# Two merge lanes become three, and the constant rows and first tokens go ahead of the first norm, in a four-layer transformer kernel

## The chip, the cores and the metric

The kernel runs on one core of one Trainium2 chip. The metric is the device time of one execution in microseconds, taken as the median over several runs; the program before the change has 2537.3 us (3 runs, 2535.52 to 2537.45). One further execution was recorded by the hardware profiler.

## The reference, cut to what is computed

Input is `x` (2 batches, 1024 tokens, 256 channels), a conditioning vector for each batch and a context of 77 tokens. Four layers follow each other, all with 256 channels and 16 heads of 16:

```python
x = L0(x)   # modulated norm, window attention (8 windows of 128 tokens, rolled by 64), projection;
            # norm, top-16 cross attention over the 77 context tokens; norm, SwiGLU MLP
x = L1(x)   # norm, attention over the context as prototypes, 3 experts, gate, x + gate * routed
x = L2(x)   # modulated norm, rotary full self attention with a block mask; cross attention; GELU MLP
x = L3(x)   # modulated norm, full self attention without a mask; cross attention; GELU MLP
```

The full self attention of L2 and L3, the part that matters most here, is for each batch and head

```python
attn = softmax(einsum('bqhd,bkhd->bhqk', q, k) * scale)      # 1024 x 1024, L2: masked first
out = einsum('bhqk,bkhd->bqhd', attn, v).reshape(B, N, 256) @ W_proj
```

## The kernel before, in words

**Stages and lanes.** The program is made of stages (`Norm`, `Parts` for the q and k projections, `Values`, `Attention`, `OutProject`, `Mlp`, `Experts` ...). Each stage has one generator for each of the five engines (tensor = PE, vector = DVE, scalar = ACT, pool = POOL, sync = the DMA queue SP). A generator issues an instruction or a few and yields. `phases` (L2855) lists the stages in columns, the lanes: lane 0 holds the attentions, lane 1 the other batch's projections, norms and MLPs, and SP has a third lane of loads. For each engine `merge` (L244) takes turns among the lanes' generators by a string in `ORDER` (L192): each character is a number of yields to take from the next lane in turn (`Z` adds 61 and stays on the lane). So the strings are the complete order of each engine, written out by hand or by a planner; nothing is decided at run time but semaphore waits.

**Batches.** While batch 0 is in an attention on lane 0, batch 1 is in its dense stages on lane 1, and the other way round.

**A full attention** (`Attention`, L1058, `kind="full"`) works on 8 groups of 2 heads. For a group and each of 32 steps: `max_tile` (L1159) makes a product of 128 queries x 512 keys in one of banks 0 and 1 (L1171), and DVE takes its row maximum (L1303; in the masked layer L1300 adds the mask too). After the 32, the maxima are transposed (L1140), split in two bf16 parts (L1257, L1260) and put by DMA as two more rows into the stacked queries (L1118). Then `exp_tile` (L1181) makes the transposed product with that shift (L1196, mask by L1200) in bank 2 or 3, ACT takes the exponential (L1238) into one of seven buffers, and `pv` (L1203) multiplies four of them with the values into bank 4 (L1224, four strips of the array side by side). After the group ACT copies bank 4 (`finish_copy`, L1027), PE transposes it (`finish_turn`, L1034) and DVE divides by the sums (`finish_out`, L1045, L1051). The turned sums go into a bank of the pair 0 and 1: line 1153 takes `self.bank("max", turns)`. All this is laid out on beats: exponentials begin 40 beats behind the maxima, value products 46, the turn 75; a group begins each 40 beats (masked layer) or 32 (last layer). Each beat ends in a yield of its own, whether or not anything was issued in it.

**The start.** `Start.sync` (L433) issues the DMAs of the condition, `ident`, `cols`, the bias and the first piece of the modulation weights, then all tokens of batch 0 in one DMA (L438), then the weights. `Mods` multiplies the condition with the modulation weights piece by piece (L554). `Norm` takes statistics of eight tiles of 128 tokens (L695, L700), POOL takes one inverse root for all eight (`root_guess`, L666 and L668), DVE refines it (L644 to L651) and normalizes tile by tile (L718), PE transposes each (L740), ACT applies the modulation into `hT` (L782). The window attention rolls the tokens by 64, so its projections (L822) need both halves of `hT`. `StackRows` (L473) fills constant rows (-1, 0, 1 in bf16) of the stacked queries and keys of three buffers, nine fills of 2048 elements, and the ones beside the values, in a single yield, in lane 1 behind the norm.

## Time and profile before

| | |
|---|---|
| median of 3 runs | 2537.3 us |
| profiled execution | 2540.68 us |
| its span, first to last instruction | 2539.4 us |
| granted TensorE clock, mean | 0.951 |
| busy: PE, DVE, ACT, POOL | 2331.7, 1686.7, 1267.6, 384.6 us |
| instructions | 37005 |
| DMA | 160.6 MB |

Busy time is the union of an engine's drawn instructions. Matmuls are pipelined and their ends are modelled, so two that follow each other closely overlap in the drawing, and a short wait can lie under a drawn product. A weight load (PEld) runs ahead of the product it belongs to, so its idle time is partly covered. Idle time of an engine is put down to what ended it.

### The profile page before, as it was taken

To read this page: it belongs to the slowest core of one execution; us is meant where nothing else is said; L and a number is where in the kernel's file an instruction comes from. 1 tells how busy PE (TensorE), PEld (TensorE's weight loads), DVE (VectorE), ACT (ScalarE), POOL (GpSimd) and SP (SyncE) were. 2 spreads that over 40 slices of the span, in tenths; PEclk is the share of its full clock that TensorE was granted. 3 is DMA by queue.
4 is the path that set the end of the run, shared out by engine and by line. 5 is a ranking of instruction groups with operands and counts; after the bars stand their busy time and mean duration, and the time that the engine had idled before them with its cause. 6 is when DMAs were issued, how large, how long until landed. Compare 5 with 4: busy or idle time off the path is not lost.

```text
span 2539.4 us, 37005 instructions
## 1 busy us (share of the span) xinstructions
PE 2331.7 (92%) x13127; PEld 1214.5 (48%) x13127; DVE 1686.7 (66%) x5146; ACT 1267.6 (50%) x2434; POOL 384.6 (15%) x407
## 2 busy tenths in 40 slices
PE   6789789978997989999989999998999989999997
PEld 2566345555554545545444455552344433334554
DVE  5666978676235575567867775758886668884563
ACT  2334445443222314455546655645766637776553
POOL 3011444244121110001110010010001010002021
PEclk8899789999998979999999999997999999999999
DMA  4666440000001140001223100042221042110120
GB/s 161 186 153 203 123 142 24 28 22 5 4 9 33 63 78 18 14 14 26 94 86 101 56 18 13 14 150 75 66 50 21 18 131 88 52 41 11 51 71 17
DMA packets 150925, 160.63 MB, mean 63 GB/s; under 512 B 33391, under 2 KB 120259, under 8 KB 150477
## 3 DMA queue, kind: packets, MB, share of 16 engines
q1 hardware_dynamic: 150740, 158.28, 22.0%
q8 instruction: 103, 1.69, 0.3%
q14 instruction: 82, 0.66, 0.1%
HBM read 97.39 MB, written 60.19 MB: 62 GB/s over the span
## 4 chain that ended last, share of the span: by engine, by line
PE 74%; DVE 13%; ACT 3%; DMA 3%; POOL 2%; issue 2%; SPq 1%; ACTq 0%; DVEq 0%; POOLq 0%
PE bank L1224 10%; PE bank L1196 9%; PE bank L1758 9%; PE bank L1171 9%; PE bank L1781 6%; PE bank L1200 4%; PE bank L822 4%; PE bank L2264 4%; PE bank L2444 3%; PE bank L1678 3%; DVE max L1303 2%; PE bank L2266 2%; PE bank L740 2%; PE bank L1034 1%; DVE stats L695 1%
## 5 line engine op out<-in xcount | busy, mean ns | idle before, releaser
L1238 ACT ACTIVATE work<-bank 128x512 f32<-128x512 f32 (+1 forms) x1216 | 687.6, 596 | 404.8 <-PE bank L1200 199.5
L1300 DVE CUSTOM_DVE_ANT_0 bank<-bank,weights 128x512 f32<-128x512 f32 x512 | 347.3, 702 | 121.3 <-PE bank L1171 119.8
L1171 PE MATMUL bank<-k_stack,q_stack 97*128 97x512 bf16 x896 | 354.6, 401 | 35.8 <-DVE max L1303 17.6
L1303 DVE TENSOR_REDUCE max<-bank 128x1 f32<-128x512 f32 x512 | 334.1, 684 | 72.5 <-PE bank L1171 70.0
L1196 PE MATMUL bank<-q_stack,k_stack 99*128 99x512 bf16 x896 | 339.9, 383 | 7.5 <-ACT work L1238 5.8
L1758 PE MATMUL bank<-hT,weights 128*128 128x512 f32 x512 | 256.4, 612 | 9.8 <-ACT work L1808 4.3
L1171 PEld LDWEIGHTS bank<-k_stack,q_stack 97*128 97x128 bf16 x896 | 88.3, 99 | 250.9 <-DVE max L1303 106.7
L1200 PEld LDWEIGHTS bank<-ident_b,weights 128*128 128x128 bf16 x2048 | 157.8, 97 | 102.0 <-issue 8.5
L1781 PE MATMUL bank<-weights,work 128*128 128x256 f32 x768 | 195.8, 384 | 3.5 <-DVE work L1848 3.2
L1200 PE MATMUL bank<-ident_b,weights 128*128 128x128 bf16 x2048 | 198.1, 218 | 0.0
L1781 PEld LDWEIGHTS bank<-weights,work 128*128 128x128 f32 x768 | 140.8, 190 | 67.4 <-issue 29.5
L822 PE MATMUL bank<-hT,weights 128*128 128x512 f32 x288 | 152.4, 644 | 9.4 <-ACT hT L782 4.7
L1196 PEld LDWEIGHTS bank<-q_stack,k_stack 99*128 99x128 bf16 x896 | 86.9, 98 | 115.9 <-ACT work L1238 73.5
L1290 DVE TENSOR_REDUCE max<-bank 128x4 f32<-128x308 f32 (+1 forms) x192 | 101.8, 544 | 51.4 <-PE bank L1177 50.5
L1224 PE MATMUL bank<-work,weights 128*17 128x512 f32 x1024 | 135.5, 598 | 0.0
L1758 PEld LDWEIGHTS bank<-hT,weights 128*128 128x128 f32 x512 | 92.8, 193 | 88.0 <-issue 57.2
L1224 PE MATMUL bank<-work,v 128*17 128x512 f32 x1024 | 134.7, 598 | 0.0
L2264 PE MATMUL bank<-hT,weights 128*128 128x512 f32 (+1 forms) x240 | 123.6, 627 | 0.5 <-ACT work L2462 0.3
L740 PE MATMUL bank<-ident,work 128*128 128x128 f32 x320 | 73.8, 346 | 48.0 <-DVE work L718 44.1
L1550 POOL TENSOR_TENSOR x<-x,row_consts 128x256 f32<-128x256 f32 x112 | 84.5, 754 | 193.2 <-DMA row_consts<-in_L_b_cproj 176.8
L2444 PE MATMUL bank<-weights,work 128*128 128x256 f32 x384 | 95.7, 385 | 1.0 <-DVE routed L2590 0.4
L2458 ACT ACTIVATE work<-bank,half_anchor 128x512 f32<-128x512 f32 x56 | 38.5, 687 | 114.6 <-PE bank L2266 112.2
(241 smaller groups left out, 3611.6 us busy)
## 6 DMA issues: line engine op xcount, KB each, us to landing
q_stack<-parts_q SPq DMA_DIRECT2D x60, 384.0 KB, 4.1
parts_q<-parts SPq DMA_DIRECT2D x46, 384.0 KB, 2.6
k_stack<-parts_k SPq DMA_DIRECT2D x40, 384.0 KB, 4.9
weights<-parts_q SPq DMA_DIRECT2D x36, 384.0 KB, 3.8
parts_q<-parts SPq DMA_DIRECT2D x46, 256.0 KB, 2.9
parts_k<-parts SPq DMA_DIRECT2D x24, 384.0 KB, 2.6
parts_k<-parts SPq DMA_DIRECT2D x24, 256.0 KB, 3.0
weights<-in_L_e_w SPq DMA_DIRECT2D x12, 512.0 KB, 7.5
```

What stands on the lines that cost most here:

```text
L822: m = pe.e.matmul(bank.ap[:, :], w[:, i, self.col + c * P:self.col + (c + 1) * P], hT[self.b][:, bl, i, :], start=i == 0, stop=i == CC - 1)
L1171: m = pe.e.matmul(bank.ap[:, :], self.q(g)[0:MAX_ROW, h, qt * P:(qt + 1) * P], k_stacks[self.key, g].ap[0:MAX_ROW, h, half * BLK:(half + 1 ...
L1196: m = pe.e.matmul(bank.ap[0:self.nk, :], self.k(g, h, STACK, kt * P), q, start=True, stop=not self.mask)
L1200: m = pe.e.matmul(bank.ap[:, j * P:(j + 1) * P], mask_bias[:, half * TPB + j, kt * P:(kt + 1) * P], ident_b[:, :], start=False, stop=j == ...
L1224: m = pe.e.matmul(o[strip:strip + DV, :], self.v[:, kt, head, :] if self.own else self.v[:, head, :], p[0:self.nk, :], start=kt == 0, stop ...
L1238: ac.e.activation(p.ap[0:self.nk, :], banks[self.key, "exp", g, i].ap[0:self.nk, :], ACT.Exp).then_inc(*probs.tick((self.key, g, i)))
L1300: ve.e.tensor_tensor_reduce(bank[:, :], bank[:, :], mask_bias[:, qt, half * BLK:(half + 1) * BLK], 1.0, -3.4e38, ALU.add, ALU.max, to).the ...
L1303: ve.e.tensor_reduce(to, bank[:, :], AX_X, ALU.max).then_inc(*maxima.tick((self.key, g, i)))
L1758: m = pe.e.matmul(banks[key].ap[:, :], w1[:, k, col:col + P], hT[self.b][:, bl, k, :], start=k == 0, stop=k == CC - 1)
L1781: m = pe.e.matmul(banks[self.key, tp].ap[:, i * C:(i + 1) * C], hid[:, at * P:(at + 1) * P], w2[:, j, :], start=(j == 0 and i == 0), stop= ...
L2264: return pe.e.matmul(out, wt[name][:, k, lo:hi], hT[self.b][:, self.bl, k, :], start=k == 0, stop=False)
L2444: m = pe.e.matmul(banks[key, "acc", ex, pair].ap[:, i * C:(i + 1) * C], hid[:, at * P:(at + 1) * P], wt[f"L1w2_{ex}"][:, j, :], start=(j = ...
```

## The change

- `Start.sync` issues batch 0's tokens as two DMAs of 512 tokens, directly behind the condition and ahead of `ident`, `cols` and the modulation weights.
- Fills of the constant rows write two bf16 values as one f32 pattern (`fill`). `StackRows` stands first in lane 1, ahead of the first norm, with one yield for each fill; the ones beside the values and the context's key rows become a stage `ValueOnes`, behind that norm.
- The first norm of batch 0 takes its inverse root in two halves (`roots=2`); each half's tiles follow its own root.
- In the four full attentions, `FullAttention` keeps the maximum products, their maxima and the turned maxima on lane 0, without empty yields. `Weighting`, in a new lane, holds the exponential products, the exponentials, the value products and the turn of the sums. The turn takes bank 4 (`pv`) in place of a bank of the maxima. The maximum bank now alternates over the maximum products and the turned maxima alone.
- PE, DVE and ACT merge three lanes; all order strings are new (that of POOL in one character).

```diff
             def sync(self, sp):
                 sp.e.dma_start(condT[:, :, :], a["condT"].rearrange("(c p) b -> p c b", p=P)).then_inc(*ld_cond.tick("condT"))
+                tokens = a["x"][0].rearrange("(t p) c -> p t c", p=P)
+                for bl in range(NB):
+                    at = slice(bl * TPB, (bl + 1) * TPB)
+                    sp.e.dma_start(x[0][:, at, :], tokens[:, at, :]).then_inc(*ld_x[0].tick(("x", bl)))
                 sp.e.dma_start(ident[:, :], a["ident"]).then_inc(*ld_cond.tick("ident"))
                 sp.e.dma_start(cols[:, :], a["cols"]).then_inc(*ld_cond.tick("all"))
                 self.mods.begin(sp)
-                sp.e.dma_start(x[0][:, :, :], a["x"][0].rearrange("(t p) c -> p t c", p=P)).then_inc(*ld_x[0].tick("x"))
...
+        PAIR_OF = {-1.0: -1.0058441162109375, 0.0: 0.0, 1.0: 1.0058441162109375}
+        def fill(po, rows, value):
+            return po.e.memset(rows.rearrange("p h s -> p (h s)").bitcast(F32), PAIR_OF[value])
...
                 for i, (q, k) in ((2, (window_q, window_k)), (0, (q_buf[0], k_buf[0])), (1, (q_buf[1], k_buf[1]))):
                     po.wait_ge(*pool_done.latest)
-                    po.e.memset(k[BIAS_ROW:STACK, :, :], -1.0).then_inc(*pool_done.tick(("k_rows", i, 0)))
+                    fill(po, k[BIAS_ROW:STACK, :, :], -1.0).then_inc(*pool_done.tick(("k_rows", i, 0)))
+                    yield
...
+        class ValueOnes(Stage):
+            def pool(self, po):
                 po.wait_ge(*pool_done.latest)
                 po.e.memset(V[:, :, :, D:DV], 1.0).then_inc(*pool_done.tick("V_ones"))
+                yield
...
+                for part in self.parts:
+                    lo, hi = part[0], part[-1] + 1
+                    yield from inverse_root(ve, (key, lo), rstd[b][:, lo:hi], newton[b][:, 0, lo:hi], newton[b][:, 1, lo:hi])
+                    ve.wait_ge(*vec[(key, lo), "root"])
...
+        class FullAttention(Attention):
+            def tensor(self, pe):
+                turns = 0
+                for beat in range(self.beats):
+                    if now := self.group(beat, 0, self.n):
+                        self.max_tile(pe, *now, turns)
+                        yield
+                        turns += 1
+                    if now := self.group(beat, self.rows_at + 1, 1):
...
+        class Weighting(Stage):
+            def tensor(self, pe):
+                attn = self.attn
+                for beat in range(attn.beats):
+                    if now := attn.group(beat, attn.exp_at, attn.n):
+                        attn.exp_tile(pe, *now)
+                        yield
+                    if now := attn.group(beat, attn.pv_at, attn.n):
+                        if now[1] % 4 == 0:
+                            attn.pv(pe, now[0], now[1] // 4)
+                            yield
+                    if now := attn.group(beat, attn.fin_at + attn.late, 1):
+                        g = now[0]
+                        bank = banks.take(attn.bank("pv", g), (attn.key, "turn", g), (vec, (attn.key, "out", g)))
+                        attn.finish_turn(pe, g, bank)
+                        yield
...
-            ([mods["L0"]], [early(0, "v")] + of(0, "n1") + [StackRows()] + of(0, "k", "q") + [begin_win] + of(0, "v"), [Rest(3), LoadTokens(1), Rest(1)]),
+            ([mods["L0"]], [StackRows(), early(0, "v")] + of(0, "n1") + [ValueOnes()] + of(0, "k", "q") + [begin_win] + of(0, "v"), [Rest(3), LoadTokens(1), Rest(1)]),
...
-            merge(ORDER["tensor"], *[itertools.chain.from_iterable(s.tensor(pe) for s in lane) for lane in lanes[0:2]])
+            merge(ORDER["tensor"], *[itertools.chain.from_iterable(s.tensor(pe) for s in lane) for lane in (lanes[0], lanes[1], lanes[3])])
```

## Rows read from the trace of the kernel before

**Rows 1.** Busy us (instructions) of PE, PEld, DVE, ACT, POOL; clock; DMA share; GB/s.

```profile
0.00:36.00 36.00, 17.32 (x40) 4.08 (x40) 24.09 (x48) 5.35 (x10) 21.02 (x21) 0.99 0.46 153
36.00:250.00 214.00, 181.86 (x1426) 126.10 (x1427) 128.14 (x331) 83.11 (x157) 19.55 (x22) 0.90 0.63 176
...
919.00:1330.00 411.00, 388.92 (x2542) 193.97 (x2540) 284.44 (x806) 195.47 (x336) 26.92 (x22) 0.95 0.16 40
1330.00:1698.00 368.00, 363.03 (x2673) 190.33 (x2672) 248.40 (x706) 222.47 (x388) 22.48 (x22) 1.00 0.19 56
1698.00:2062.00 364.00, 341.39 (x1751) 143.90 (x1750) 267.61 (x554) 226.22 (x410) 25.65 (x29) 0.96 0.24 65
2062.00:2337.00 275.00, 260.86 (x1474) 93.70 (x1473) 216.56 (x445) 180.45 (x334) 24.58 (x32) 0.97 0.17 47
```

**Rows 2.** Order of time in the last layer's second attention: start, us, instruction.

```profile
2201.45 1.05 PE L1224 MATMUL bank<-work,weights 128*17 128x512 f32 x8
...
2202.44 0.39 PE L1171 MATMUL bank<-k_stack,q_stack 97*128 97x512 bf16 x1
...
2202.66 0.38 PE L1196 MATMUL bank<-q_stack,k_stack 99*128 99x512 bf16 x1
...
2203.32 0.60 PE L1034 MATMUL bank<-ident,work 128*128 128x128 f32 x4
...
2205.66 0.49 DVE L1051 TENSOR_TENSOR hT<-bank,den 128x128 f32<-128x128 f32 x2
```

**Rows 3.** Waits over the whole span: who for whom, us in total, times, longest.

```profile
PEld bank L1171 <- DVE max L1303: 134.6, 231, 3.8
DVE bank L1300 <- PE bank L1171: 119.8, 125, 4.3
...
PEld bank L1171 <- DVE max L1300: 85.1, 104, 3.9
...
DVE max L1303 <- PE bank L1171: 70.0, 117, 2.2
...
DVE den L1045 <- PE bank L1034: 58.5, 45, 5.2
```

**Rows 4.** The maximum products' group, and one line of their waits.

```profile
L1171 PE MATMUL bank<-k_stack,q_stack 97*128 97x512 bf16 x896 | 354.6, 401 | 35.8 <-DVE max L1303 17.6 <-DVE max L1300 14.5 <-DVE hT L1051 0.8
...
  DVE hT L1051: 6.5, 13
```

**Rows 5.** Order of time in the head.

```profile
3.03 0.46 SPq L438 DMA_DIRECT2D x<-in_x  x1
...
6.49 3.57 PE L554 MATMUL bank<-weights,scondT 128*2 128x512 f32 x4 [6.49 <-DMA weights<-in_L_w_ada]
...
10.79 0.73 DVE L695 BATCH_NORM_STATS2 stats<-x 128x6 f32<-128x256 f32 x2
...
16.43 1.80 POOL L478 MEMSET weights<- 3x2048 bf16 x1
...
17.01 7.05 DVE L718 TENSOR_SCALAR work<-x,mean_var,rstd 128x256 f32<-128x256 f32 x4
...
28.82 1.88 PE L554 MATMUL bank<-weights,scondT 128*2 128x512 f32 x4
...
36.02 9.99 PE L822 MATMUL bank<-hT,weights 128*128 128x512 f32 x16 [2.02 <-ACT hT L782]
```

**Rows 6.** Order of time: the norm of batch 1, beside the window attention.

```profile
77.82 0.73 DVE L718 TENSOR_SCALAR work<-x,mean_var,rstd 128x256 f32<-128x256 f32 x2
```

**Rows 7.** POOL's groups by shape: count, busy us, mean ns.

```profile
L668 POOL TENSOR_TENSOR rstd<-newton,minus_half 128x4 f32<-128x4 f32 x12 | 13.3, 1112 | 1.0
...
L492 POOL MEMSET kx_stack<- 3x1232 bf16 x2 | 2.2, 1119 | 0.1
...
L478 POOL MEMSET weights<- 3x2048 bf16 x1 | 1.8, 1799 | 0.1
...
L485 POOL MEMSET v<- 128x128 f32 x1 | 0.4, 352 | 0.1
```

More of the change, by code:

```diff
@@ L684, in __init__ @@
                 self.lead = len(self.tiles) // 2 + 2
+                n = len(self.tiles) // roots
+                self.parts = [self.tiles[k * n:(k + 1) * n] for k in range(roots)]
                 self.z_done = evac if name in ("L2n2", "L3n2") and blk is None else vec
@@ L1244, in scalar, with exponentials @@
                     yield
+            def exponentials(self, ac, g, i):
+                p = work[self.key, "prob", g, i]
+                for f in p.free:
+                    ac.wait_ge(*f)
+                ac.wait_ge(*exp_scores[self.key, g, i])
+                ac.e.activation(p.ap[0:self.nk, :], banks[self.key, "exp", g, i].ap[0:self.nk, :], ACT.Exp).then_inc(
+                    *probs.tick((self.key, g, i)))
             def vector(self, ve):
@@ L1303, in max_of, with scalar, vector @@
                     ve.e.tensor_reduce(to, bank[:, :], AX_X, ALU.max).then_inc(*maxima.tick((self.key, g, i)))
+        class FullAttention(Attention):
[4 more added lines that the diff above has]
+                        self.max_tile(pe, *now, turns)
+                        yield
+                        turns += 1
+                    if now := self.group(beat, self.rows_at + 1, 1):
+                        g = now[0]
+                        bank = banks.take(self.bank("max", turns), (self.key, "rows", g), (vec, (self.key, "rows", g)))
+                        for f in bank.free:
+                            pe.wait_ge(*f)
+                        pe.wait_ge(*maxima[self.key, g, "rows"])
+                        pe.e.transpose(bank.ap[0:PAIR * NT, 0:P], max1[self.key, g].ap[:, :], ident[:, :]).then_inc(
+                            *turned.tick((self.key, "rows", g)))
+                        yield
+                        turns += 1
+            def scalar(self, ac):
+                return iter(())
+            def vector(self, ve):
+                for beat in range(self.beats):
+                    if now := self.group(beat, self.rows_at + 2, 1):
+                        yield from self.rows_of(ve, now[0])
+                    if now := self.group(beat, 0, self.n):
+                        self.max_of(ve, *now)
+                        yield
+                    if now := self.group(beat, self.rows_at, 1):
+                        self.both_halves(ve, now[0])
+                        yield
@@ L2894, in sync_program @@
         def sync_program(sp):
-            merge(ORDER["sync"], *[itertools.chain.from_iterable(s.sync(sp) for s in lane) for lane in lanes])
+            merge(ORDER["sync"], *[itertools.chain.from_iterable(s.sync(sp) for s in lane) for lane in lanes[0:3]])
             sp.wait_ge(*st_out["all"])
```

243 lines of the change are left out of this document (144 added, 99 removed).

## The prediction

> **What bounds the kernel now.** I read the busy times by stretch first [rows 1], to see where PE is not fed. Until 36 us it works 17.3 us and POOL 21.0. The rest of the first layer (36 to 250 us) has PE at 182 of 214. The four full attentions fill 919 to 2337 us: there PE reads 94 to 99% busy, but a 512-column bf16 product is drawn with 0.39 us and the next starts 0.22 us later [rows 2], so up to 0.17 us of a wait hides under each drawn product. DVE, which takes the maxima, is busy 268 of 364 us and 217 of 275 us in the two attentions of the last layer. So the middle is two engines that wait for each other through two PSUM banks, and the waits say so [rows 3]: DVE waits for the maximum products 119.8 us (masked layer) and 70.0 us (last layer), PE's weight loads wait for the maxima 85.1 and 134.6 us, while PE itself stands drawn idle for this only 17.6 + 14.5 us [rows 4].
>
> The next view is the order of time of the head [rows 5]. The tokens' DMA goes out at 3.03, behind five others; the first statistics run at 10.79. From 16.43, right behind the norm's root, POOL fills the constant rows. The first four normalized tiles take 7.05 us, 1.76 each, while the next norm's tile takes 0.37 (two in 0.73) [rows 6]. So POOL's fills set the pace of DVE's L718. The Trainium skill, "SBUF — State Buffer", Who interferes with whom, says the same of a `tensor_scalar` beside a GpSimd instruction: whoever starts first holds the shared pair for its whole length; by that rule, the trace agrees. The first projection (L822) starts at 36.02.
>
> **Head, part by part.** (1) Tokens earlier: two DMAs of 512 KB go out second and third, near 1.2 and 1.7 us. The old 1 MB took from 3.03 to 10.79, behind 0.5 MB of modulation weights and shared with 0.75 MB; the halves should be there by 6 to 7 us. What they are moved past pays: ident, cols and the first modulation weights come behind 1 MB, some 1.5 to 2.5 us later (first product 6.49 -> about 8.5). DVE must do its casts (behind cols) before the statistics, so these start near 7.5 and the eight end near 11. (2) The fills now run first on POOL, from about 0.8 us, in nine pieces, and the first root waits for them in POOL's order. Each piece is half as many elements, because two bf16 are written as one f32. By element, the fills of 2048 and 1232 elements [rows 7] give (1.80 - 1.12)/816 = 0.83 ns each and 0.10 fixed: 0.95 us for 1024, nine with gaps 9.1 us, done at 9.9. By byte each stays at 1.83: 16.9 us, done near 17.7. The only f32 fill of size, 128 elements in 0.35 us, fits bytes rather better (0.10 + 256 x 0.83 ns = 0.31) but steps over 17 elements. I take 0.95, the contiguous rows, and keep 1.83. The Trainium skill has "a memset takes one cycle per element whatever the dtype" ("VectorE: DVE Perf Modes", Zero memsets can be issued as uint32); it is said of the other engine, and no row here shows it of POOL; by it the fill would be about 1 us. (3) The root is split. The first half has 4 columns; the statistics of tile 3 are there near 9, so root (1.11, POOL's 4-column row [rows 7], and its variance before) ends at 11.4 and DVE's three steps at 12.0. (4) New order on PE: one modulation piece, tiles 0 and 1, a piece, tiles 2 and 3, a piece, tiles 4 to 7, a piece, then L822. A piece took 3.57 us at 6.49 and 1.88 at 28.82 [rows 5]. From 12.0: tiles 0 and 1 by 13.5, piece to 17.1, tiles to 18.5, piece to 22, tiles (0.4 to 0.5 us each undisturbed, some under V's fills) to 24.5, ACT L782 to 26.5, L822 near 27. With pieces at 1.88 all along it is 23. So the **head** gains 36.0 - 27 = 9 us, at best 13. If fills cost by byte, the same chain starts 8 us later and the gain is 0 to 2. Behind L822 the chain is products, casts and DMAs that wait for each other, with nothing clocked from outside (the DMA engines are at 63% in that stretch [rows 1]), so I let the 9 us through to the end.
>
> **Full attentions.** The arithmetic is unchanged: each of 1024 tile pairs still has its product, maximum and exponential. I read the order strings with the units each stage yields. The coarse order is the old one: the exponential products begin 33 to 39 maximum products behind, groups start within some 20 units of the neighbour lane's work. What is new is fine. (a) Two maximum products in a row stand 71 and 58 times in the last layer's attentions, 20 and 20 before: both banks are full before four value products hold PE (eight records, 0.99 us from their start to the next product [rows 2]). (b) The 32 turns of the sums leave the maximum banks and go to bank 4. Now a turn holds such a bank from 2203.32 to 2206.15, 2.8 us [rows 2]. The weight loads of L1171 waited 6.5 us in all for such reads [rows 4]. I take 5, bounds 0 and 6.5. (c) Order: the visible 32.1 us of PE, and 335 waits of its weight loads, each hiding up to 0.17 us, 57 us: 32 to 89 us are open to it. I take 10, a tenth to a third of that, bounds 0 and 30, since DVE is idle for 21 to 33% of these stretches [rows 1] and PE's real load leaves less. (d) Against it: bank 4 now carries the value sums, then their turn. The first value product of the next group stands on PE behind DVE's read of the turn (L1051), and behind it all of PE's queue. In the last layer the new order has 1 to 4 maximum products, 3 exponential products and 0 to 8 units of the neighbour between: 1.1 us and more, for a chain of 2.8. I take half of the 14 hand-overs at 0.7 us, 5 us, bounds 0 and 36 (28 x 1.3, the mean wait of L1045 [rows 3]). Sum: 5 + 10 - 5 = **10 us** gained.
>
> The remaining edits have one answer. KeyRows' and QueryRows' halved fills lie on POOL under attention work; at most 8 x 0.9 us, hidden, 0. The early layers' order is refitted (PE's lane position differs by at most 34 units); nothing in it has a sign: 0, within 8 us.
>
> **Sum.** The profiled execution took 2540.7 us (span 2539.4 and 1.3 around it), 3.4 above the median of the runs. 2540.7 - 9 - 10 = 2521.7; on the median's scale 2537.3 - 19 = **2518**.
>
> **Rivals.**
> *Bytes.* Fills at 1.83 us: the head gives 0 to 2 and the rest 8 to 10: 2526. For it the 128-element f32 row, against it the contiguous ones.
> *Bank 4.* Slower. Each of the 28 hand-overs stops PE at the first value product until L1051 is done. Price 1.0 to 1.3 us each, 28 to 36 us, minus the head's 9: 2537.3 + 22 = 2559. It decides from about 0.7 us per hand-over (19 us lost, both gains gone). For it: two maximum products plus three exponential ones are 1.1 us against 2.8. Against it: the masked layer has 4 to 8 of each between, and probability buffers for seven tiles let ACT go on.
> *The order works.* Pairs keep DVE fed: a third of its 190 us of waits comes off: -63, of which PE's own load lets through about 40: 2537.3 - 9 - 40 = 2488.
> *Nothing moves.* The head's gain is lost in the first attention of batch 0, whose waits are DMA round trips with their own order, and the fine order is neutral: 2535.
>
> **How the numbers follow.** Forecast 0.48, bytes 0.13, the order works 0.14, nothing moves 0.14, bank 4 0.11. Two in a thousand, 5 us, is about what a measurement tells. Faster takes the first three, 0.75; nothing moves is the same, 0.14; bank 4 is slower, 0.11. The forecast's own range by its bounds (head 0 to 13, attentions -5 to +25, early order 8 either way, not all at once) is 2500 to 2530; the range reaches to the order case and to no change: 2487 to 2541. Bank 4 and the far side of the order case lie outside.
>
> **What would show it.** In the changed profile L695 starts near 7.5 us, the fills of 1024 f32 last 0.95 us and end before 10, L718 takes about 0.5 us each, L822 starts near 27; the first windowed product comes 9 us sooner. In the last layer DVE's wait for L1171 falls from 70.0 and that for L1300 from 119.8. A weight load or product of the values that waits for L1051 would be the bank-4 case: under 10 us in all by my forecast, over 25 by the rival. I am wrong if the head's lead is gone by 250 us, if the fills last 1.8 us, or if the attentions' stretch (919 to 2337, 1418 us) is not shorter by 3 to 25 us.

## The result and the profile after

| | before | after |
|---|---|---|
| median of the runs | 2536.8 us | 2476.1 us |
| profiled execution | 2540.7 us | 2470.1 us |
| its span | 2539.4 us | 2467.9 us |

The changed kernel is faster: the ratio is 0.976, with a 95% interval of 0.9739 to 0.9781. That is 61 us where 19 were forecast, and outside the range of 2487 to 2541. The profiled execution was the fastest of its four; the others had spans of 2474.4 to 2478.5. The two traces differ by 71.5 us: about 6 of these belong to this one execution after, which ran below its median, and 4 to the one before, which ran above.

The stretches that answer to [rows 1], with their borders put at nearly the same work. The columns are as there.

```profile
0.00:23.14 23.14, 13.21 (x40) 3.66 (x40) 15.44 (x50) 5.35 (x10) 16.94 (x26) 1.00 0.66 226
23.14:225.00 201.86, 168.86 (x1401) 117.42 (x1400) 125.81 (x322) 80.51 (x149) 19.17 (x23) 0.94 0.63 176
...
869.00:1279.00 410.00, 389.96 (x2563) 198.82 (x2561) 281.47 (x796) 190.82 (x333) 27.00 (x22) 0.95 0.16 41
1279.00:1646.00 367.00, 363.99 (x2679) 189.99 (x2678) 255.01 (x717) 223.64 (x395) 21.67 (x22) 1.00 0.19 58
1646.00:1999.00 353.00, 339.37 (x1763) 145.92 (x1763) 269.35 (x560) 225.83 (x410) 24.76 (x29) 0.98 0.24 67
1999.00:2265.00 266.00, 255.19 (x1480) 93.96 (x1478) 219.41 (x447) 179.42 (x334) 21.91 (x30) 0.99 0.18 51
```

The head is 12.9 us shorter (36.0 to 23.14). The stretch that began at 919 now begins at 869. The two stretches of the masked layer are as long as before (411 and 368, now 410 and 367). The two of the last layer are 11 and 9 us shorter. So 50 us are won ahead of the attentions and 20 in the last layer. In the second stretch (214 us before, 201.9 now) PE's idle time is as it was, 32 and 33 us; its drawn time fell from 182 to 169. Some 6 of these 13 us are 25 products that now stand behind the border (1401 for 1426); the rest goes with a granted clock of 0.94 in place of 0.90.

The head in order of time, with the instructions that answer to [rows 5]:

```profile
0.88 2.95 POOL L512 MEMSET weights<- 3x1024 f32 x3
1.21 1.01 SPq L470 DMA_DIRECT2D x<-in_x  x2
...
8.45 0.75 DVE L749 BATCH_NORM_STATS2 stats<-x 128x6 f32<-128x256 f32 x2
...
9.15 3.57 PE L606 MATMUL bank<-weights,scondT 128*2 128x512 f32 x4 [9.15 <-DMA weights<-in_L_w_ada]
...
10.67 1.04 POOL L720 TENSOR_TENSOR rstd<-newton,minus_half 128x4 f32<-128x4 f32 x1
...
12.45 0.73 DVE L775 TENSOR_SCALAR work<-x,mean_var,rstd 128x256 f32<-128x256 f32 x2
...
17.05 1.88 PE L606 MATMUL bank<-weights,scondT 128*2 128x512 f32 x4
17.09 2.85 DVE L775 TENSOR_SCALAR work<-x,mean_var,rstd 128x256 f32<-128x256 f32 x3
...
23.14 7.13 PE L881 MATMUL bank<-hT,weights 128*128 128x512 f32 x16
```

Three fills take 2.95 us, so 0.98 each with their gaps. The first normalized tiles take 0.37 us each, as [rows 6] had it, and 0.95 each from 17.09, where POOL fills two rows of kx (1.12 us and 1.16 us). The statistics start at 8.45 though the tokens landed 4.1 to 5.2 us after their issue, by 7: DVE had first to do its casts, which waited for `cols` until 7.30. Before, too, the tokens were not what the statistics waited for. They stood behind L585, and that for PE:

```profile
10.18 0.68 DVE L585 TENSOR_TENSOR weights<-bank,weights 2x512 f32<-2x512 f32 x1 [4.27 <-PE bank L554]
```

The old token DMA landed 6.4 us after its issue, near 9.4.

The waits that answer to [rows 3]; L1230 is the old L1171, L1361 and L1364 are L1300 and L1303, L1104 is L1045, L1093 is L1034:

```profile
DVE bank L1361 <- PE bank L1230: 148.4, 157, 4.7
...
PEld bank L1230 <- DVE max L1364: 93.4, 185, 4.9
...
PEld bank L1230 <- DVE max L1361: 64.4, 93, 4.9
...
DVE max L1364 <- PE bank L1230: 52.6, 107, 1.9
...
DVE den L1104 <- PE bank L1093: 40.6, 30, 6.6
```

PE's weight loads wait 62 us less for the maxima (134.6 + 85.1 to 93.4 + 64.4). In the last layer DVE waits 17 us less. In the masked layer it waits 29 us more, and the layer is no shorter and no longer for it; so DVE does not seem to set the pace there.

### The profile page after: what moved, and what is told of

It reads as the page before. It is cut to its first block, busy times and chain, and to the rows that moved or that the text cites. A ratio compares the mean times of both kernels' runs of the same rounds, so it can differ in the third digit from the quotient of the medians.

```text
span 2467.9 us, 37021 instructions
## 1 busy us (share of the span) xinstructions
PE 2297.5 (93%) x13127; PEld 1208.8 (49%) x13127; DVE 1676.6 (68%) x5149; ACT 1258.8 (51%) x2434; POOL 370.1 (15%) x409
## 4 chain that ended last, share of the span: by engine, by line
PE 76%; DVE 11%; DMA 3%; ACT 3%; POOL 3%; issue 2%; SPq 1%; DVEq 0%; ACTq 0%; POOLq 0%
PE bank L1283 11%; PE bank L1255 10%; PE bank L1891 9%; PE bank L1230 9%; PE bank L1914 6%; PE bank L1259 4%; PE bank L2397 4%; PE bank L881 3%; PE bank L2577 3%; PE bank L1811 3%; PE bank L2399 2%; PE bank L797 2%; PE bank L1093 1%; PE bank L2559 1%; DVE stats L749 1%
## 5 line engine op out<-in xcount | busy, mean ns | idle before, releaser
L1304 ACT ACTIVATE work<-bank 128x512 f32<-128x512 f32 (+1 forms) x1216 | 679.9, 595 | 393.7 <-PE bank L1259 196.0
L1361 DVE CUSTOM_DVE_ANT_0 bank<-bank,weights 128x512 f32<-128x512 f32 x512 | 348.1, 704 | 149.7 <-PE bank L1230 148.4
L1364 DVE TENSOR_REDUCE max<-bank 128x1 f32<-128x512 f32 x512 | 334.7, 684 | 55.8 <-PE bank L1230 52.6
L1230 PE MATMUL bank<-k_stack,q_stack 97*128 97x512 bf16 x896 | 333.0, 396 | 33.4 <-DVE max L1364 15.4
L1255 PE MATMUL bank<-q_stack,k_stack 99*128 99x512 bf16 x896 | 333.9, 384 | 5.4 <-ACT work L1304 2.8
L1891 PE MATMUL bank<-hT,weights 128*128 128x512 f32 x512 | 255.4, 611 | 7.3 <-ACT hT L841 3.7
L1259 PEld LDWEIGHTS bank<-ident_b,weights 128*128 128x128 bf16 x2048 | 157.9, 97 | 93.1 <-issue 10.4
L1914 PE MATMUL bank<-weights,work 128*128 128x256 f32 x768 | 196.8, 385 | 3.7 <-DVE work L1981 3.2
L1230 PEld LDWEIGHTS bank<-k_stack,q_stack 97*128 97x128 bf16 x896 | 86.0, 99 | 183.3 <-DVE max L1364 75.5
L881 PE MATMUL bank<-hT,weights 128*128 128x512 f32 x288 | 145.5, 617 | 9.5 <-ACT parts L904 5.1
L1722 POOL TENSOR_TENSOR x<-x,work 128x512 f32<-128x512 f32 x24 | 31.4, 1307 | 456.5 <-DVE work L1711 454.9
L797 PE MATMUL bank<-ident,work 128*128 128x128 f32 x320 | 71.9, 341 | 26.2 <-DVE work L775 23.5
```

The lines of the kernel that those rows point to most:

```text
L797: m = pe.e.transpose(banks[key, bl, c].ap[:, i * P:(i + 1) * P], work[key, "z", t].ap[:, c * P:(c + 1) * P], ident[:, :])
L881: m = pe.e.matmul(bank.ap[:, :], w[:, i, self.col + c * P:self.col + (c + 1) * P], hT[self.b][:, bl, i, :], start=i == 0, stop=i == CC - 1)
L1230: m = pe.e.matmul(bank.ap[:, :], self.q(g)[0:MAX_ROW, h, qt * P:(qt + 1) * P], k_stacks[self.key, g].ap[0:MAX_ROW, h, half * BLK:(half + 1 ...
L1255: m = pe.e.matmul(bank.ap[0:self.nk, :], self.k(g, h, STACK, kt * P), q, start=True, stop=not self.mask)
L1259: m = pe.e.matmul(bank.ap[:, j * P:(j + 1) * P], mask_bias[:, half * TPB + j, kt * P:(kt + 1) * P], ident_b[:, :], start=False, stop=j == ...
L1304: ac.e.activation(p.ap[0:self.nk, :], banks[self.key, "exp", g, i].ap[0:self.nk, :], ACT.Exp).then_inc(*probs.tick((self.key, g, i)))
```

## The experiments

Each was timed beside runs of the kernel before on the same chip. "Gain" is the distance of the medians, in us. The interval of a ratio is some 0.15 to 0.35% to either side, 4 to 9 us, so that two gains less than 6 to 12 us apart can't be told apart by the medians alone. Places in a trace are those of one execution, which can lie 5 us off its median. The order strings are cut into three regions: *head* (through the first norm), *early* (to the first full attention) and *late*.

**One part alone.** The order strings of the old and the new kernel hold nearly the same units. So each region can be taken from either. For instance the first line of PE's string, old order behind the head (as in e17) and new:

```diff
     "tensor": (
-        "1903202403c01102d0110fc0720210210450460820j20620110h10v10430120420840920720a20ck0310620410220730410Q90510g10310c2042"
+        "1903202403d03301b0b90210220710230310260920220l20720c20710a20210j20j207208207407705i0920410220730410Q90510g10310c2042"
```

e1: the head's edits and order only. e2: these and the new early order. e3: the new early order alone. e4: the third lane, bank 4 and the late order alone.

> The head alone: earlier tokens, constant rows first and filled as f32, the root in two halves, and the new order of the first projection; every other order string and the attentions as before. Theory A (the head's 13 us are carried and nothing more; the other 48 us come from the new orders): 2524 us. Theory B (the head's lead also brings the waits of the first 500 us down, and the order strings have no part in that): 2490 to 2500. Rival of the prediction (the lead is lost later): 2535.

> The head and the new order of all engines up to the first full attention; the four attentions with their old code, bank and order. Theory A: head 13 and early order 32, 2537 - 45 = 2492. If the later order gives all of the rest by itself, the full change is 27 us below this.

> The new order between the head and the first full attention alone: head, attentions and everything else as before. Theory A: 2537 - 32 = 2505. Theory B (the early gain belongs to the head's lead): 2530 to 2537.

> The third lane with its order, bank 4 for the turn and the new order from the first full attention on; head and all earlier order as before. Theory A (gains add up): 2537 - 27 = 2510. My prediction's term: 10 us, 2527. Theory C (the late gain is there only because batch 1 arrives earlier): 2535.

Measured: e1 2522.4, a gain of 16.5 (ratio 0.994, 0.9918 to 0.9961); e2 2504.6, 34.4; e3 2522.7, 16.2; e4 2523.6, 15.3. The early order is a term of its own, of the size of the other two. Head and early order add up (16.5 + 16.2 against 34.4). All three make 48.0, the whole change 60.7; the 13 that are left, known to some 11 us either way, are taken up below ("What the parts don't add up to"). The expectations had read 32 us for the early order and 27 for the late one off the traces; e2, e3 and e4 came 12 to 18 us above their first theory.

**The whole change without the early order.**

> The changed kernel with the old order of the early layers: new head, new order from the first full attention on, everything between in the order of before. What is open: head plus early order gave 34.4 us and the late part alone 15.3, together 49.7, while the whole change gave 62.8; and 13 us of it were won around the first full attention, where the run with head and early order had lost its lead. Theory 1 (the early order is a term of its own, 16 to 18 us, and the late part is worth 28 only where head and early order stand before it): 16.5 + 15.3 = 32, so about 2507 us with before at 2539, the lead at the first maximum product near 18. Theory 2 (the late order gets its extra 13 us from the head's lead or from the clock, not from the early order): 2539 - 16.5 - 28 = about 2494. Theory 3 (the orders were fitted as one; half of it is a loss): above 2515.

Measured: 2502.2, a gain of 37.4, nearest to theory 1. So taking the early order out costs 23 (60.7 - 37.4) in the whole change. Where it does so is seen in three stretches. They end at the same work (2701 and 2705 products of PE are done by the second border, 3908 and 3904 by the last). They don't begin at it: by 231 e5 has done 1467, the changed kernel by 223 only 1426, so its 8 us of lead there are little more than work put off. The first two hold most of the top-k stage (L1525 runs from 226 to 592 in e5, 222 to 564 after); the third ends 11 us behind the masked layer's first maximum (907 and 871). First e5, then after:

```profile
231.00:392.00 161.00, 133.50 (x607) 73.09 (x607) 131.35 (x829) 72.92 (x218) 71.18 (x82) 0.84 0.37 118
392.00:543.00 151.00, 135.22 (x632) 83.94 (x630) 106.15 (x687) 73.47 (x208) 58.20 (x64) 0.90 0.10 28
543.00:918.00 375.00, 345.53 (x1209) 204.38 (x1206) 189.26 (x563) 110.66 (x215) 77.17 (x78) 0.94 0.14 33
```

```profile
223.00:376.00 153.00, 132.81 (x646) 75.60 (x645) 132.16 (x856) 74.58 (x228) 70.56 (x80) 0.89 0.42 135
376.00:516.00 140.00, 127.30 (x637) 79.32 (x635) 107.15 (x697) 75.31 (x217) 59.17 (x64) 0.95 0.11 34
516.00:882.00 366.00, 344.04 (x1201) 206.49 (x1200) 182.65 (x538) 109.97 (x209) 73.72 (x76) 0.94 0.13 32
```

Together 687 us became 659; PE's idle time fell from 73 to 55, and its drawn time from 614 to 604, at a higher granted clock. (These two executions lie 36 us apart, their medians 26.) The waits of PE that fell, from its waits in the first two stretches, first e5, then after:

```profile
PE bank L1537 <- POOL k_stack L1616: 11.8, 8, 3.6
PE bank L797 <- DVE work L775: 11.7, 6, 6.5
```

```profile
PE bank L797 <- DVE work L775: 4.8, 5, 3.4
PE bank L1537 <- POOL k_stack L1616: 1.6, 5, 0.7
```

L1537 turns the top-k exponentials once POOL has masked them (L1616). L797 turns the tiles of a norm. Two of them, in e5's order of time:

```profile
325.28 1.14 PE L1537 MATMUL bank<-ident,k_stack 128*77 128x128 f32 x4 [3.62 <-POOL k_stack L1616]
...
540.46 1.09 PE L797 MATMUL bank<-ident,work 128*128 128x128 f32 x4 [6.47 <-DVE work L775]
```

In these 3.6 and 6.5 us all of PE's queue stands behind one unit (what a lane issues between two yields).

**Parts of the early order** (all else as in the changed kernel). e11: new until batch 1's window attention begins. e12: new on SP alone. e14: new on PE, DVE and ACT, old on SP. e15: new in that window attention only. e17: new from its start on. The edit is of the kind shown, in the lines that hold the region. The expectations place this window attention at 230 to 370 us; by the trace it is over by 218 (the last L1252 of its shape starts at 217.6 in e5), and what they describe there is the top-k stage.

> The changed kernel with the new early order only until the window attention of batch 1 begins (near 240 us) and the old order from there to the first full attention. With the old order all the way it was 2502, with the new one 2476. Theory 1 (the waits that fell were those of batch 1's window attention and of the top-k stage at 240 to 540 us: PE for its scores' copies 12.0 to 1.5 us, vector for the turns 15.4 to 1.7): the first part brings little, 2495 to 2502. Theory 2 (the lead comes from batch 0's first products and the order of loads): 2480 to 2488. Theory 3 (a fitted order is worth only whole): slower than 2502.

> The changed kernel with the old order of PE, vector and scalar up to the first full attention, and the new order there for the DMA queue of SP alone. Theory 1 (the 26 us of the early order are PE's in-order stalls, which fall with the order of PE, vector and scalar): 2500 to 2503, no change from the 2502 of the run without the early order. Theory 2 (the round trips through DRAM are issued earlier, and that is the gain): 2476 to 2486. Halfway would say that both are needed.

> The changed kernel with the old order of SP's DMA queue up to the first full attention and the new order of PE, vector and scalar. SP's new order alone had made it 15 us slower than the old one. Theory 1 (the gain is the engines' order, SP's has only to follow it): 2476 to 2482. Theory 2 (the two have to fit): an issue that stands in the old place holds back what the engines now want earlier, 2490 to 2510.

> The changed kernel with the new early order only in the window attention of batch 1 (from its first unit to the first unit of the top-k stage, near 230 to 370 us), the old order before and behind it. With none of it 2502, with all 2476. Theory 1 (the window stage carries it: there PE is busy 133 of 161 us in the run without it, 133 of 153 with it, and the granted clock reads 0.84 against 0.89): 2488 to 2492. Theory 2 (the gain is in the top-k stage, PE 135 of 151 against 127 of 140, and behind): 2498 to 2502.

> The changed kernel with the old order between the head and the start of batch 1's window attention, and the new order from there on. Theory 1 (the whole of the early order's gain lies behind that start): within 4 us of the changed kernel, 2472 to 2480. Theory 2 (the order before it prepares the gain, since neither part gives any alone): 2490 to 2502.

| | gain | PE's wait at L1537, L797 |
|---|---|---|
| e5, none of it | 37.4 | 11.8, 11.7 us |
| e11, before window 1 | 34.6 | 11.0, 12.5 |
| e15, window 1 only | 32.6 | 11.1, 11.9 |
| e12, SP only | 20.9 | 10.4, 11.7 |
| e14, all but SP | 49.0 | 6.2, 2.4 |
| e17, from window 1 on | 61.2 | 1.3, 5.5 |
| whole change | 60.7 | 1.6, 4.8 |

The waits are those between 231 and 543 us in e5, and of the same work in the others. Every run that keeps both lacks the gain, and every run that has lost them has it. The same holds for the runs of one part: the two waits are 10.4 and 12.5 us in e1 and 11.0 and 11.7 in e4, where the early order is old, and 1.5 and 5.9 in e3 and 1.4 and 6.5 in e2, where it is new and gives 16 and 18.

What lies before the window attention gives nothing that can be told (e11), nor does that attention (e15), and all from its start on gives everything (e17): so the gain is in the top-k stage and behind it. SP's new order alone costs 16 us against e5. Most of that lies ahead of the top-k stage: in e12 the window attention's products end at 232, in e5 at 218. Without SP's new order the engines' order reaches 12 of the 23, between the two theories of e14. So the two have to fit.

That the two waits cause the gain isn't shown by a run of its own: no kernel moved these units and nothing else. And the runs that keep them while the late order is new (e5, e11, e12, e15) differ from the whole change in a second thing as well, which is told below; so of the 23 us only the 16 to 18 of e3 and e2 can be put down to the early order by itself.

**Bank 4 and the late order.** e6 puts the turn of the sums back into the banks of the maxima, with the new order; vector's reads of a turn move up by as many as 19 places of DVE's order where the next maximum needs the bank.

```diff
-                        bank = banks.take(attn.bank("pv", g), (attn.key, "turn", g), (vec, (attn.key, "out", g)))
+                        bank = banks.take(attn.bank("max", attn.turns), (attn.key, "turn", g), (vec, (attn.key, "out", g)))
                         attn.finish_turn(pe, g, bank)
+                        attn.turns += 1
```

> The whole change, but the turn of each group's sums goes through a bank of the maxima again, as before, and not through bank 4; vector's three reads of the turn stand where the maximum that takes this bank next needs them. Term (b) of the forecast: bank 4 for the turns is worth 5 us, bounds 0 and 6.5, so 5 us slower than the changed kernel, about 2481. Rival (order alone): within 2 us of the changed kernel, 2474 to 2478; bank 4 only frees the order from a deadlock and gives no time itself. Rival (the banks are the gain): most of the attentions' 19 to 28 us goes, 2495 to 2504; weight loads of the maximum products then wait again for the reads of the turn.

Measured: 2505.2, a gain of 34.5: 26 less than the whole change, and as much as head and early order have without any late part (e2, 34.4). The trace shows the wait itself:

```profile
PE bank L1230 <- DVE hT L1110: 16.7, 17, 1.5
```

PE stands idle 16.7 us, in 17 waits, for DVE's read of a turn; in the changed kernel L1230 never does. PE in the last layer's second attention of e6, around one turn, with DVE's part of it:

```profile
2188.51 0.66 PE L1093 MATMUL bank<-ident,work 128*128 128x128 f32 x4
...
2189.49 0.39 PE L1230 MATMUL bank<-weights 97*128 97x512 bf16 x1
...
2190.81 0.49 DVE L1110 TENSOR_TENSOR hT<-bank,den 128x128 f32<-128x128 f32 x2
2191.36 0.39 PE L1230 MATMUL bank<-weights 97*128 97x512 bf16 x1 [1.15 <-DVE hT L1110]
```

The bank is taken from 2188.5 to 2191.3, 2.8 us as in [rows 2], and PE stands idle 1.15 us for it. In the changed kernel the same three steps pass beside products of both kinds and a run of value products:

```profile
2130.61 0.60 PE L1093 MATMUL bank<-ident,work 128*128 128x128 f32 x4
2131.05 0.38 PE L1255 MATMUL bank<-q_stack,k_stack 99*128 99x512 bf16 x1
2131.27 0.38 PE L1230 MATMUL bank<-k_stack,q_stack 97*128 97x512 bf16 x1
...
2132.06 1.05 PE L1283 MATMUL bank<-work,weights 128*17 128x512 f32 x8
2132.29 0.25 DVE L1104 RECIPROCAL den<-bank 128x16 f32<-128x16 f32 x1
2132.57 0.49 DVE L1110 TENSOR_TENSOR hT<-bank,den 128x128 f32<-128x128 f32 x2
```

**The price of the hold by itself.** In e9 (e2, so with the old attentions and their order), e10 (the changed kernel) and e13 (the changed kernel with the turn in the maximum banks) DVE reads a constant tile in place of the turned sums, so the bank is free once PE has written it. These kernels leave the result of the full attentions out. e9 differs from e2 in nothing else. e13 differs from e6 also in DVE's order, which is the changed kernel's, without the reads that e6 had to move up. The edit of e10:

```diff
-                v4 = banks[self.key, "turn", g].ap[:, :].rearrange("p (t a d) -> p t a d", t=TPB, a=4)
...
+                    v4 = minus_half[:, 0:TPB].unsqueeze(2).unsqueeze(3).to_broadcast([P, TPB, 4, 32])
...
-                        bank = banks.take(attn.bank("pv", g), (attn.key, "turn", g), (vec, (attn.key, "out", g)))
+                        bank = banks.take(attn.bank("pv", g), (attn.key, "turn", g), (turned, (attn.key, "sum", g)))
```

> Head and early order (2504.6 us), the old full attentions with their old order and the turn in the banks of the maxima, but vector's three steps behind each of the 32 turns read a constant tile in SBUF in place of the turned sums, so the bank is free when PE has written it. The output of the full attentions is left out of the result this way (a constant in its place); every instruction is still there. Open: the turn in the maximum banks costs 28 us with the new order (2476 against 2505), where I had 5 for it, bounds 0 and 6.5, from the waits of the kernel before. Theory 1 (each turn holds a bank for 2.8 us of vector's chain in any order, and its price was hidden among the waits for maxima): 32 x 0.9 = 28 us off, about 2477. Theory 2 (my 5 was right for the old order, in which the fitted distances cover the hold; only the new order, fitted without the hold, is hurt by it): 0 to 7 off, 2498 to 2504.

> The changed kernel, with the same substitution: vector's steps behind the 32 turns read a constant tile in SBUF, so bank 4 is free for the next group's value sums as soon as PE has turned the sums (output of the full attentions replaced by a constant). It prices the hand-over of bank 4, which the forecast put at 5 us (14 of 28 hand-overs at 0.7), bounds 0 and 36. Theory 1 (hidden): within 2 us of the changed kernel, 2474 to 2478. Theory 2 (5 us as forecast): 2471. Rival bank 4 in a milder form: 10 us and more off, below 2466.

> The new order with the turn of the sums in the banks of the maxima (that was 2505), but vector's steps behind the 32 turns read a constant tile, so such a bank is free as soon as PE has written it (output of the full attentions replaced by a constant). Theory 1 (the 28 us are the hold of 2.8 us on a maximum bank, which the new order leaves no room for): 2476 to 2480, as with bank 4. Theory 2 (bank 4 as such, or the reads of the turn that were put earlier on vector, make the difference): 2495 to 2505.

| attention's order | turn in the maximum banks, read | the same, freed early | turn in bank 4, read | the same, freed early |
|---|---|---|---|---|
| old | 34.4 (e2) | 36.1 (e9) | not tried | |
| new | 34.5 (e6) | 52.7 (e13) | 60.7 | 60.6 (e10) |

In the old order the hold costs 2 us, which is not to be told from nothing. In the new one hold and moved reads together cost 18, and the 16.7 us of PE's idle time in e6 say that the hold is nearly all of it. The next value sums' wait for bank 4 costs nothing (60.7 against 60.6). So the new order is worth 17 to 26 us, and only where a turn doesn't hold a maximum bank; bank 4 without the new order would by e9 have been worth about 2 (an estimate). That e13 stays 8 us behind e10 is at the edge of what the medians tell, and open. The empty square wasn't tried: by the order strings the engines would wait for each other in a ring with the old order and bank 4, but no run shows it.

**Pairs, and the last layer alone.** e7 exchanges, on PE only, the second maximum product of 89 pairs with the exponential product behind it (M, x, V: maximum, exponential, value products):

```
changed kernel  ...xxMMVMMxx-MMxxM...
e7              ...xMxMVMxMx-MxMxM...
```

> The whole change, but on PE alone 89 pairs of maximum products (maximum, maximum, exponential) are put as maximum, exponential, maximum; the other engines keep their order. Term (a) of the forecast: pairs fill both banks ahead of the value products. If that is what the fine order brings, the attentions give back most of their 19 us: 2490 to 2495. If the gain is where the neighbour lane's work and the exponentials stand, the swaps cost little: 2476 to 2480. Halfway is possible, since a fitted order is disturbed by any swap of one engine: about 0.2 us for each of 89 swaps would be 18 us as well, and vector's waits for L1230 tell it: they would rise from 52.6 us in the last layer toward 70.

> Head, early order, turns in the maximum banks with vector reading a constant (as in the runs of 2503 with the old and 2482 with the new order of the attentions), with the old order through the masked layer and the new one in the last layer only. Theory 1 (the traces: last layer's first maximum to the end took 828 us in the old, 817 in the new order, the masked layer 778 and 779, and 10 us come with the earlier first maximum of the masked layer): 2490 to 2494. Theory 2 (the masked layer's new order prepares the last layer): 2500 to 2503. Theory 3 (the masked layer's order brings nothing at all, also not before its first maximum): 2480 to 2484.

e7: 2484.1, a gain of 55.6, 5 below the whole change, which the intervals don't tell from nothing (0.9762 to 0.9802 and 0.9739 to 0.9781). DVE's wait in the last layer rose by 4 us (52.6 to 56.7), not to the 70 of the kernel before. By the medians the pairs are no more than a third of the order's worth. e18 (e13 with the old order through the masked layer): 2496.1, a gain of 42.6, between 36.1 (e9) and 52.7 (e13). From the last layer's first maximum to the end the traces have 839.7 us in e9, 827.4 in e13 and 827.4 in e18; there the last layer's part is whole by itself. Between the first maximum of the masked layer and that of the last one all three have 778 or 779, as before (777). The rest of e13's lead lies at the masked layer's first maximum (887.5 in e9, 876.7 in e13 and 892.0 in e18): the new order draws its first group forward.

**The head's two parts.** e8 fills the rows as bf16 again, e16 loads the tokens of batch 0 in one DMA behind the modulation weights again.

```diff
-            return po.e.memset(rows.rearrange("p h s -> p (h s)").bitcast(F32), PAIR_OF[value])
+            return po.e.memset(rows, value)
```

```diff
-                tokens = a["x"][0].rearrange("(t p) c -> p t c", p=P)
-                for bl in range(NB):
-                    at = slice(bl * TPB, (bl + 1) * TPB)
-                    sp.e.dma_start(x[0][:, at, :], tokens[:, at, :]).then_inc(*ld_x[0].tick(("x", bl)))
...
+                sp.e.dma_start(x[0][:, :, :], a["x"][0].rearrange("(t p) c -> p t c", p=P)).then_inc(*ld_x[0].tick("x"))
```

> The whole change, but the constant rows are filled as bf16, so twice the elements in each fill (1.83 instead of 0.95 us). Of the rows in the head nine fills end near 17.8 instead of 9.9 us; the first norm's root waits for them in POOL's order. Theory 1 (the head is bound by this chain, and its lead reaches the end): all is 7 to 8 us later at the first projection, the end near 2484. Theory 2 (by 10 us PE has its four modulation pieces to do, 1.9 us each and one of 3.6, so the chain has slack and DVE's normalized tiles would run beside fewer fills): first projection 4 us later, the end 2476 to 2480. Theory 3 (the fills under the attentions matter too): more than 10 us, 2487 and above.

> The changed kernel with the tokens of batch 0 again in one DMA of 1 MB, behind the modulation weights, as in the kernel before; fills, the split root and the order stay new. The fills (9.9 us) no longer set the start then: the tokens were there at 10.8 us before, so the statistics start near 10.8 in place of 8.45, the first root near 13.5 in place of 10.4. Theory 1 (the chain through the root sets the first projection): 3 us later there and at the end, 2479, and with the clock as in the other runs up to 2484. Theory 2 (PE's modulation pieces set it): within 1 us, 2474 to 2478.

e8: 2491.0, 12 less gain (48.7). Its fills and what waits for them:

```profile
15.73 1.80 POOL L512 MEMSET q_stack<- 1x2048 bf16 x1
18.02 1.04 POOL L720 TENSOR_TENSOR rstd<-newton,minus_half 128x4 f32<-128x4 f32 x1
...
31.59 7.13 PE L881 MATMUL bank<-hT,weights 128*128 128x512 f32 x16
```

The first projection is 8.5 us later, as in theory 1, and the end 12 us by the medians, as in theory 3. e8 also doubles the fills under the attentions; what these cost by themselves wasn't tried, and the 3.5 us between the two readings are within the scatter. e16: 2473.7, a gain of 61.1. The statistics start at 9.31 in place of 8.45 and the first projection at 24.62 in place of 23.14:

```profile
9.31 0.75 DVE L746 BATCH_NORM_STATS2 stats<-x 128x6 f32<-128x256 f32 x2 [2.38 <-DMA x<-in_x]
```

so the early tokens are worth 1.5 us at the first projection, and nothing that a run can tell at the end.

**What the parts don't add up to.** The traces put the 13 us at one place. The row from the start to the masked layer's first maximum (L1300, or what it became), for the kernel before, e4, e2 and after:

```profile
0.00:921.00 921.00, 800.62 (x3895) 485.94 (x3895) 569.65 (x2421) 345.38 (x807) 249.47 (x263) 0.92 0.30 85
0.00:926.00 926.00, 806.90 (x3895) 489.19 (x3895) 569.52 (x2422) 346.14 (x807) 249.34 (x263) 0.91 0.29 84
0.00:884.00 884.00, 784.15 (x3895) 480.06 (x3895) 556.13 (x2425) 345.06 (x807) 238.87 (x265) 0.93 0.30 88
0.00:871.20 871.20, 774.34 (x3855) 473.70 (x3856) 550.76 (x2415) 341.55 (x802) 236.80 (x264) 0.94 0.30 89
```

With the early order old, the late order makes this first maximum 5 us later (e4 against before, and 907 in e5 against 903 in e1); with the early order new, 13 us sooner (after against e2). In the last layer it wins as much either way (841.4 to 818.9 us in e4, 839.0 to 818.6 behind e2). That is 18 us in single traces for the 13 of the medians. The rows show what differs: PE has 3855 products ahead of that maximum in place of 3895. The 40 are products of the experts, 8.5 us as drawn. They stand behind the first maximum there, and the masked layer takes no longer for them (778.1 us with 5252 products, 777.3 with 5210 in e2). All kernels in which both the late order and PE's early order from window 1 on are new have 3855, and all others 3895, e5, e11, e12 and e15 among them. So this piece belongs to both orders at once, and it is in the 23 us of e5 as well. No run moved these 40 products alone.

**The clock.** A part of the 13 us may be the clock. The four runs of the changed kernel had mean granted clocks of 0.961, 0.956, 0.956 and 0.956 for spans of 2467.9 and 2474.4 to 2478.5. Over all runs on record, each compared with the others of its kernel and chip, 0.001 of mean clock goes with 1.2 us. The two levels are 1.2 and 2.4 GHz, so a mean of 0.951 over 2538 us (before) is 249 us at the lower one, and 0.956 over 2475 is 218: 31 us less, where e4 has 11 us more. If PE loses half of such time (an estimate, and a high one, since PE doesn't bound every stretch and it makes 2.5 us of each 0.001), the kernels stand without it at 2413 (before), 2399 (e1), 2403 (e3), 2391 (e4) and 2368 (after). Then the three parts alone give 14 + 10 + 22 = 46, and the whole 45. But by the same estimate head and early order no longer add up (14 + 10 against 18 in e2), and with the 1.2 us of the scatter the parts give 47 and the whole 54. No run held the clock fixed, so how much of the 13 us is clock stays open.

## Why the prediction was wrong

**Head: mechanism right, 9 us forecast, 16.5 measured (e1).** The fills cost by element and end at 9.86 (forecast 9.9). The first projection came at 23.14: the "23 with pieces at 1.88 all along", and not the 27 taken. The mis-sized term is PE's pieces: after the first one (3.57 us) they took 2.23 and 1.88, where each had been charged 3.57, which is 3 of the 4 us. The value of the early tokens, told at length, was 1.5 us there and nothing at the end (e16). It had been read wrongly: 10.79 was taken for the landing of the old DMA, and was the end of L585, which had waited for PE. The fills were most of it, 8.5 of the 12.9 us at the first projection (e8). The rest of the 16.5, 3.6 us, is won behind the head, and by the estimate above 2 of it is clock.

**Early order: the step that failed.** "Nothing in it has a sign: 0, within 8 us" was read off how far units had moved (34 at most), and not off the waits that could fall. PE stood idle 12.0 us for POOL L1483 and 12.0 for the norm's tiles between 239 and 557 us before. The order gave 16 (e3) and 18 (e1 to e2), and 23 (e5 to the whole) with the piece that it shares with the late order. The sum had 19 us and 60.7 came. Of the 42 that it lacks, the early order by itself is 16, the piece that only head, early and late order together give 13, the head 7.5 and the attentions by themselves 5 (e3, the whole, e1, e4). That second piece failed with the same step: the sum added its terms as if each edit were worth the same whatever stands beside it.

**Attentions: 10 forecast, 26 measured (e2 to the whole change), 15 alone (e4).** With head and early order in place they passed even the upper bound of 25, if barely. (a) Pairs are worth about 5, in the noise. (b) The turns' hold was put at 5 and is 2 in the old order (e9): right for the kernel that the rows came from, and wrong as a term of the sum, since with the new order the hold costs up to 18 (e6 to e13), of which 16.7 are seen as PE's wait. The 6.5 us of waits bounded the price in the old order only. (c) The order was given 10 of 32 to 89 us; it is worth 17 to 26. (d) The hand-over of bank 4 was charged 5, and is 0 (e10). In the stretch of the attentions (869 to 2265) PE and its weight loads wait 8 us for L1110, the value products 3.3 of them, as forecast (under 10).

**Where in the attentions.** The forecast had DVE's wait for L1300 fall from 119.8; it rose to 148.4, and the masked layer kept its time. The last layer's wait for L1303 fell from 70.0 to 52.6 as forecast, and the time with it: 841.4 us from its first maximum to the end became 818.6, with 11 us less of PE's idle time and 12 less of its drawn time. In the masked layer's two stretches PE stands idle for 20 and 3 us, as before (22 and 5); there the order won nothing. The sign named in the prediction, that the stretch of 1418 us be 3 to 25 us shorter, held (1396, 22 less): what failed lies ahead of it.

**The rivals.** *The order works* gave 2488 and was nearest, but by another way: it had 40 us in the attentions, where 26 came, and none in the early layers. *Bytes* and *bank 4* fell with e8 and e10, *nothing moves* with e1. None had the early order at more than 8 us, so even the lowest case ended 12 us too high.

## What to carry to other kernels

A refitted order of in-order engines is a term with a size: before it is put at zero, list the waits at which the bound engine stands idle behind a unit that could stand later, stage by stage, and take their sum as the open end. (Here that was 24 us for 16 to 18 won; that these waits were the cause is likely, not shown.) Two orders that meet at a border can be worth more together than apart: 13 us here, at the place where the first group of an attention begins. A buffer's hold costs what the order around it lets it cost, 2 us here and up to 18: measured in the old order it doesn't bound its price in the new one, so price buffer and order as one edit. And of a stage, ask first whether its busiest engine has any idle time left; only there can fewer waits elsewhere shorten it.

## What the runs showed of the hardware

- POOL's fill costs by element: 1.80 us for 2048 bf16 (e8) and 0.98 with its gap for 1024 f32, of the same 4096 bytes on a partition. The Trainium skill has a memset's time by element of the other engine ("VectorE: DVE Perf Modes", Zero memsets can be issued as uint32); for POOL these rows show it.
- A fill beside DVE's normalization stretches it: 0.37 us a tile alone, 0.95 beside fills of 1232 elements (after, from 17.09), 1.76 beside fills of 2048 [rows 5].
- The granted clock of a stretch moved with the order of the work. In the first two of the three stretches above 0.84 and 0.90 became 0.89 and 0.95, with 10 us less of PE's idle time; over all three the drawn time fell by 10 us (614 to 604). In the rest of the first layer 0.90 became 0.94 with PE's idle time unchanged (32 and 33 us) [rows 1]. Less waiting doesn't always go with it: e4 has less of it in the last layer and the lower mean clock (0.946 to 0.950, before 0.949 to 0.955). What raises it isn't shown.
